# First layer's router scores by rows: the turned rows of a tile standing, the router's eight columns moving

## The reference

```python
def _L0_ffn_ref(X, routing_W, expert_bias, sW1, sb1, sW2, sb2, rW1, rb1, rW2, rb2):
    shared = jax.nn.silu(X @ sW1 + sb1) @ sW2 + sb2
    logits = jnp.einsum('btd,ed->bte', X, routing_W) + expert_bias
    activation = jnp.sqrt(jax.nn.softplus(logits))
    top_vals, top_idx = jax.lax.top_k(activation, K)          # K = 2
    ...
    hdn = jax.nn.silu(jnp.einsum('nd,edh->enh', Xf, rW1) + rb1[:, None, :])
    y = jnp.einsum('enh,ehd->end', hdn, rW2) + rb2[:, None, :]
    routed = jnp.einsum('ne,end->nd', cf, y).reshape(B, T, d)
    return shared + routed

x = x + _L0_xattn_ref(ctx_1024, _layernorm(x), ...)
x = x + _L0_ffn_ref(_layernorm(x), ...)
x = x + _L1_xattn_ref(_layernorm(x), ctx_1024, ctx_1024, ...)
x = x + _L1_ffn_ref(_layernorm(x), ...)
```

## Time and profile before

| | us |
|---|---|
| median of 3 runs | 826.47 |
| the three runs | 830.29, 826.28, 826.47 |
| span of the profiled execution | 827.7 |
| PE busy | 767.8 (93%) |
| PE weight loads busy | 662.7 (80%) |
| DVE busy | 501.6 (61%) |
| ACT busy | 487.8 (59%) |
| POOL busy | 424.7 (51%) |
| score products, 16 recorded in the first stretch | 7.5 busy |
| ACT copies of the scores, 8 | 0.59 each |

### The profile page before, as it was taken

How to read it: one execution, slowest core, us unless ns; L and a number is a source line. 1 busy time by engine, 2 the same in 40 slices (tenths; PEclk the granted TensorE clock), 3 DMA queues, 4 the chain that set the end, 5 groups by cost and what they waited for, 6 DMA issues and landing times.

```text
span 827.7 us, 16421 instructions
## 1 busy us (share of the span) xinstructions
PE 767.8 (93%) x4472; PEld 662.7 (80%) x4472; DVE 501.6 (61%) x1360; ACT 487.8 (59%) x1374; POOL 424.7 (51%) x399
## 2 busy tenths in 40 slices
PE   4899997989898599999999999789999999999998
PEld 3646645767776499999998998679999999999997
DVE  5777856652666388788888978676222222244236
ACT  2437746655566578888778787354444444444442
POOL 3000765555686767888655788534552354322221
PEclk9989999999999899999999999899999999999999
DMA  8999996887799973553620434613444433355347
GB/s 257 345 297 336 324 312 218 263 250 222 174 251 215 299 210 84 133 123 85 177 63 1 134 136 147 201 56 116 136 135 142 134 104 103 104 181 185 121 144 232
DMA packets 128362, 147.94 MB, mean 179 GB/s; under 512 B 10747, under 2 KB 120214, under 8 KB 127254
## 3 DMA queue, kind: packets, MB, share of 16 engines
q1 hardware_dynamic: 102512, 106.02, 42.1%
q0 software_dynamic: 18624, 34.29, 15.7%
q10 hardware_dynamic: 7142, 6.59, 2.5%
HBM read 73.46 MB, written 73.40 MB: 177 GB/s over the span
## 4 chain that ended last, share of the span: by engine, by line
PE 73%; DVE 12%; DMA 4%; ACT 4%; issue 3%; DVEq 2%; SPq 0%; POOL 0%; ACTq 0%; POOLq 0%
PE psum L806 26%; PE psum L1096 9%; PE psum L1118 9%; PE psum L1184 6%; PE psum L1189 6%; PE psum L1185 6%; PE psum L1106 3%; PE psum L1198 3%; DMA fx<-xs_dram 2%; ACT pr L1485 2%; PE psum L1166 2%; PE psum L992 2%; DVE xstats L1665 1%; DVE prl L2227 1%; PE psum L1080 1%
## 5 line engine op out<-in xcount | busy, mean ns | idle before, releaser
L726 POOL DMA_INDIRECT yk_dram<-ys,L x52 | 52.1, 1003 | 144.6 <-ACT ys L1558 144.5
L673 POOL DMA_INDIRECT X<-yl_dram,slots_y x64 | 101.2, 1581 | 37.7 <-issue 13.3
L2308 DVE TENSOR_TENSOR hs<-psum,hs 128x384 f32<-128x384 f32 x71 | 39.7, 559 | 125.1 <-PE psum L1189 119.1
L645 POOL DMA_INDIRECT xs_dram<-N,slots x64 | 65.5, 1023 | 95.9 <-DVEq L1858 58.8
L1485 ACT ACTIVATE pr<-psum,nmx 128x64 f32<-128x64 f32 x512 | 108.4, 364 | 9.1 <-DVE nmx L2212 9.0
L1184 PE MATMUL psum<-whi,xTh 128*128 x284 | 109.7, 386 | 2.2 <-ACT xTh L1538 2.2
L806 PE MATMUL psum<-w_sb,cz 128*128 x426 | 103.7, 380 | 0.6 <-ACT ys L1558 0.4
L1185 PE MATMUL psum<-wlo,xTh 128*128 x284 | 96.0, 338 | 0.0
L714 POOL DMA_INDIRECT xs_dram<-N,slots x64 | 66.9, 1045 | 40.0 <-ACT ys L1558 23.3
L806 PEld LDWEIGHTS psum<-w_sb,cz 128*128 128x128 f32 x426 | 75.5, 190 | 8.4 <-issue 1.0
L1189 PE MATMUL psum<-whi,xTl 128*128 x284 | 74.0, 341 | 1.8 <-DVE xTl L2331 1.8
(11 more groups left out here) (360 smaller groups left out, 1850.1 us busy)
## 6 DMA issues: line engine op xcount, KB each, us to landing
fx<-xs_dram SPq DMA_DIRECT2D x80, 130.0 KB, 3.4
xs_dram<-fill SPq DMA_DIRECT2D x4, 2600.0 KB, 15.9
yl_dram<-fy SPq DMA_DIRECT2D x80, 128.0 KB, 3.2
xs<-xs_dram SPq DMA_DIRECT2D x71, 130.0 KB, 2.1
wlo<-in_L_ffn_W_dram SPq DMA_DIRECT2D x4, 1536.0 KB, 8.3
xs_dram<-cz SPq DMA_DIRECT2D x1, 5200.0 KB, 21.3
xs_dram<-cz SPq DMA_DIRECT2D x8, 650.0 KB, 6.7
X<-in_x_dram SPq DMA_DIRECT2D x4, 1024.0 KB, 11.9
```

The source lines that it names most:

```text
L645: po.indirect_dma_start(XS, bass.IndirectOffsetOnAxis(ap=slot[k][:, t:t + 1], axis=0), N0[:, t, :], None).then_inc(s[done], 16)
L673: po.indirect_dma_start(X[:, t, :], None, YL[b // 2], bass.IndirectOffsetOnAxis(ap=slot_y[k][:, t:t + 1], axis=0), compute_op=ALU.add).the ...
L726: po.indirect_dma_start(YK, bass.IndirectOffsetOnAxis(ap=yid[:, j:j + 1], axis=0), ys[j % YB], None).then_inc(s[f"y_out{j % YB}"], 16)
```

## The change

In `scores(g)` on TensorE the two operands change places. For each of a quad's four tiles and each half of the 256 numbers, the 128x128 turned rows stand and the 8 columns of the router move; the result is 128 partitions x 8 columns, written at once to the tile's columns of bank 4. `turn`, the ACT function `logits` with its copies and the buffer lgT0 are gone, and with them the semaphores l_lg and l_lt. The products of quad q raise l_tn, on which `choose(g)` waits as it did. Two waits of the sends get other semaphores.

```diff
@@ gpsimd: send @@
                     if (k, t) == (1, 4):
-                        po.wait_ge(s["l_lt"], LQ + 2)
+                        po.wait_ge(s["l_xa"], LQ + 3)
                     if (k, t) == (1, 8):
-                        po.wait_ge(s["l_lt"], 2 * LQ)
+                        po.wait_ge(s["l_tn"], 2 * LQ)
@@ tensor: scores @@
-                def turn(q):
-                    pe.wait_ge(s["l_lt"], q + 1)
-                    for t in range(QT):
-                        u = q * QT + t
-                        last = nc.tensor.transpose(bank[4][:, u * E:u * E + E], lgT0[q % 2][:, t * P:t * P + P], ident[0:E, 0:E])
-                    last.then_inc(s["l_tn"], 1)
...
                     pe.wait_ge(s["l_xa"], q + 1)
                     pe.wait_ge(s["l_xd"], q + 1)
-                    if q >= q0 + 2:
-                        pe.wait_ge(s["l_lt"], q - 1)
-                    for c in range(DC):
-                        last = mm(bank[3 + 2 * (q % 2)][0:E, :], roT[0][:, c, :], xT4[:, q % LQ, c, :], c == 0, c == DC - 1)
-                    last.then_inc(s["l_lg"], 1)
-                    if q > q0:
-                        turn(q - 1)
-                turn(q0 + LQ - 1)
+                    for t in range(QT):
+                        u = q * QT + t
+                        for c in range(DC):
+                            last = mm(bank[4][:, u * E:u * E + E], xT4[:, q % LQ, c, t * P:t * P + P], roT[0][:, c, :], c == 0, c == DC - 1)
+                    last.then_inc(s["l_tn"], 1)
@@ scalar: scores @@
-                def logits(q):
-                    ac.wait_ge(s["l_lg"], q + 1)
-                    if q >= 2:
-                        ac.wait_ge(s["l_tn"], q - 1)
-                    act(lgT0[q % 2], bank[3 + 2 * (q % 2)][0:E, :], ACT.Copy).then_inc(s["l_lt"], 1)
...
-                    if q > q0:
-                        logits(q - 1)
-                logits(q0 + LQ - 1)
```

More of the change, by code:

```diff
@@ L194, in build @@
         convw_sb = sb("convw_sb", [P, RATE, DC, D], stack=s1)[:, :, :, :]
-        lgT0 = [convw_sb[0:E, k, :, :].rearrange("p c n -> p (c n)") for k in range(2)]
         cu = sb("cu", [P, 2, 2, D], stack=s1)
@@ L294, in build @@
             b2_in b2_lo b2_zero sw_in rw_in
-            l_sa l_sb l_sc2 l_w2 y_back y_late l_nr l_tp l_xa l_xd l_lg l_lt l_tn l_ev l_su l_hs l_sy l_xu
+            l_sa l_sb l_sc2 l_w2 y_back y_late l_nr l_tp l_xa l_xd l_tn l_ev l_su l_hs l_sy l_xu
             f_tp f_xt f_h f_hs f_y f_ys
```

## The result

The changed kernel takes 831.59 us (median of 20 runs, 828.26 to 833.95) where the kernel before takes 828.42 us (20 runs, 823.84 to 835.27) on the same chip. The ratio is 1.0041, 95% interval 1.0026 to 1.0056: 3.4 us slower, near the 830.8 us forecast. That is within the half per cent that I took as no change, but the interval lies above 1, so the loss is clear of the noise. The time of the kernel before rests here on 20 runs; the first three of them, from which I started, had a median 2 us lower.

The account below looks back on a forecast made before the run. TensorE, busy 93% of 827.7 us, was taken as the bound. With its clock falling, 2.4 + 1.1 + 0.8 = +4.3 us on the 826.47 us median gave 830.8 us, range 822.8 to 835.5.

Parts of the forecast that it names:

- The clock falls behind narrow products: Main case, chance 0.50: TensorE's clock halves in both score stretches, +4.3 us, giving 830.8 us.
- The cost of +2.4 us: First score stretch: clock falls before the last quad's turnings, L at 68.0 instead of 65.63 us (+2.4 to +0.9).
- The full-clock prices: Score stretches at full clock: product block 1.76 us; L 1.53 us earlier in the first, 1.98 in the second.
- rival 2: Score products: clock holds but strided columns cost 0.15 us each, 2.4 us a block; +0.3 us, 826.8 us; chance 0.05.
- The second stretch: Second score stretch: clock falls over the last two blocks, -1.98 + 3.04 = +1.1 us (-2.0 to +3.5).
- the term at the rank product: Behind the second score stretch: 3.5 us of low clock, of which about 0.8 us reach VectorE.
- the one said to be hidden: Low clock behind the first score stretch: costs nothing, hidden by 1.06 us of TensorE idle before the second.
- Queues: Sends behind the second choice land in busier DMA queues and lose 0.3 us of the gain (0 to 1.1).
- rival 1: Both score stretches: TensorE's clock holds, L comes earlier twice, -3.2 us, 823.3 us (822.5 to 824.5); chance 0.30.

Follow-up runs that it names:

- c2: The changed kernel, with no further edit, run and profiled again on one chip with the kernel before; ratio 1.0036 against the kernel before.
- e1: The changed kernel with each score product moving the router's 8 columns sixteen times over (128 columns); ratio 0.9979 against the kernel before.
- e7: The same kernel as e1 (changed kernel, 128 columns moving), run again in another group; ratio 0.9992 against the kernel before.
- e5: The changed kernel with each score product moving the router's 8 columns four times over (32 columns); ratio 1.0020 against the kernel before.
- c1: The kernel before, unchanged, run and profiled again as a control; ratio 0.9988 against the other runs of the kernel before.
- e8: The kernel before with two of eight 650 KB zero fills issued after the first six loads of expert rows; ratio 1.0032 against the kernel before.
- e9: e7 with two of eight zero fills issued after the first six loads of expert rows; ratio 1.0020 against the kernel before.
- e6: The kernel before with new products only for each score stretch's last quad, 128 columns moving; ratio 0.9993 against the kernel before.
- e4: The kernel before with new products, 8 columns moving, only for the last quad of each score stretch; ratio 0.9956 against the kernel before.
- e10: The same kernel as e4 (new products only for each stretch's last quad), run again in another group; ratio 0.9967 against the kernel before.

## Why the prediction came out as it did

**The clock falls behind narrow products: right.** It was the likeliest case, at 0.50. L in the first stretch was put at 68.0 us, 16.2 behind the first turning; it came at 68.40, 15.9 behind, and 15.7 in c2. The cost of +2.4 us measured +2.1 and +1.9. That how much moves decides, which I had argued from the earlier trace rows alone, is shown by e1, e7 and the second stretch of c2. By the idle-gap rule of the Trainium skill ("TensorE: Matmul & The Clock Gate", "HAM oscillation") alone the clock would have held there; the trace disagrees, with PE busy 7.00 of 7.00 us ahead of c2's fall at 119.2 us.

**The full-clock prices: right.** Where the clock held, in after's second stretch, L came 11.02 us behind the first turning, 2.4 less than before. I had summed -1.98 for an unchanged start; the 0.4 us more are half at the front of the stretch, where the first products start 2.00 us behind the first turning in place of 2.23, and half in the turnings, of which eight take 0.91 us behind narrow products (115.03 to 115.94) in place of 1.02. The strided columns bring a block to 1.81 us from start to start (113.22 to 115.03), close to the 1.76 of the sum and far from the 2.4 of rival 2, which falls.

**The second stretch: mis-sized.** The term was +1.1 us (the fall covers the last two blocks). It measured -2.4 in one profile and -0.4 in the other: the fall came right behind the stretch, or within the first of the last two blocks. The range of -2.0 to +3.5 had the place open; I chose a middle that lay 1.5 to 3.5 us too high.

**Behind the stretches: the term at the rank product right, the one said to be hidden wrong.** The 0.8 us for the rank product measured 0.5 and 1.7. The keys and values behind the first stretch ran at the low clock until 74.2 us, and I called that hidden by the 1.06 us of idle in the earlier trace rows. In after it was not: the rank product stood at 74.73, the second stretch began 0.9 us later behind its L, released by ACT and not by VectorE. In c2, whose fall was 3.4 us shorter, it was hidden (+0.03).

**Queues: the term that was too small.** I gave 0.3 us (0 to 1.1) for sends that land in busier queues. The wait that took their place is the first load of sent rows, which is issued when the last send has landed. The DMA share by stretch, before and then after:

```profile
76.00:80.00 4.00, 4.00 (x17) 2.76 (x16) 3.18 (x15) 3.66 (x8) 0.00 (x0) 1.00 1.11 356
...
132.00:134.00 2.00, 2.00 (x7) 1.03 (x6) 1.48 (x8) 1.65 (x2) 0.00 (x0) 1.00 0.13 30
```

```profile
76.00:80.00 4.00, 4.00 (x18) 3.19 (x17) 3.52 (x12) 3.90 (x7) 0.00 (x0) 1.00 0.41 138
...
132.00:134.00 2.00, 1.28 (x7) 1.21 (x8) 1.64 (x7) 1.06 (x3) 0.96 (x1) 1.00 1.01 410
```

Two things meet here. The engines that move data are nearly full until about 128 us in the kernel before, and the low clock behind the first stretch starved them for once: 138 GB/s in place of 356 from 76 to 80 us, since the stores wait for copies of products that PE made late (the store queue waited 6.4 us for one copy, 2.4 at most before). What was not moved then is moved at the end, where the queues run full until 134 us. Before, the first load was issued 11.7 us behind L; after, 14.6; c2 13.7; e5 15.2; e7 15.9. In before, 1.6 us of PE's idle time stood ahead of the first expert product, and a load that comes later than that is paid: 2.0 us in e5, 0.4 in after. In c2 PE reached the loads late by itself: it had waited 2.01 us for ysh, as in after (0.91 before), and fell to the low clock once more at 136.3 us, which makes the 1.5 us of that step.

Counted from the start of the last send, the two causes come apart. The load is issued 2.5 to 2.9 us behind it in before, c1, c2, e1, e8 and e9, and 4.8 to 6.1 us behind it in after, e5, e6 and e7. So in c2 the load is late because the sends are; in after and e5 it is late behind the sends, with the queues full. e6 shows the second cause without the first: it has no fall of the clock up to there and lies on the chip of the result, but everything in it comes early, since the clock had not fallen near 44 us either. Its last send starts at 128.1 us and its first load at 133.2 (before: 130.1 and 132.6), and PE waits for it:

```profile
135.38 0.96 PE L1000 MATMUL psum<-ident,fx 128*128 128x128 f32 x4 [2.24 <-DMA fx<-xs_dram]
```

When the sends come early, the backlog does not end earlier. That speaks against the full -3.2 us of rival 1 even at full clock. The ratios can't say: e1 and e7, which had nearly the low clock of the kernel before, came out 0.2% and 0.1% below it, within their uncertainty, and their second stretches were disturbed.

**The sum.** Forecast +4.3 us on a base of 826.47, measured +3.4 us (2.2 to 4.6) on 828.42. The steps up to the first expert product give +1.5 and +4.8 in the two pairs, so two profiles do not fix which terms make up the +3.4. The forecast of the change was 0.9 us too high and the base 2 us too low; the second stretch was too dear, and the late load and the late start of the second stretch, which I had nearly at nothing, made up for part of it. That the total came so close is in part luck.

## What to carry to other kernels

Turning a product round so that 8 columns move and 128 stand can save time by the instruction and lose it by the clock: look at what is fed to TensorE per weight load over the whole stretch, and count what follows the stretch at half speed too. In these runs such products paid, if anywhere, where a copy and a turning back end the path, with dense work around them (e4, e10). And before a gain ahead of a load is counted, look whether the DMA engines are full there: in e6 and e7 the sends came earlier and the backlog did not end earlier.

## What the runs showed that I had not expected

A block of 32 columns behind a 128-column load takes the same time as one of 8 (1.94 and 1.92 us for 16), and lost the clock in the same place of the first stretch. In the second it kept it (1.00 from 108 to 132 us), where after lost it at 122.0 and c2 at 119.2 us.

On two of three chips the kernel before was 1.6 and 2.0% slower (842 and 846 us against 829), and in the profiles there, semaphores from TensorE came late in the busiest DMA stretch. In e1 the row turnings of two quads are recorded as done by 109.9 us, and the copies that wait for them alone start at 110.72, and at 114.35:

```profile
107.57 2.29 PE L898 MATMUL psum<-ident,N 128*128 128x128 f32 x16 [1.09 <-issue]
...
110.72 0.60 ACT L1319 ACTIVATE xT<-psum 128x512 f32<-128x512 f32 x1 [1.99 <-PE psum L898]
114.35 0.60 ACT L1319 ACTIVATE xT<-psum 128x512 f32<-128x512 f32 x1 [3.03 <-remote]
```

VectorE's copies of the same quads start at the same two moments. The page names the second releaser only as "remote". On the chip of the result such copies start within 0.3 us of the turnings' end. What delays them was not tested. It is in the old kernel's order too (e8), but no ratio can be cleared of it, and it made the second stretches of seven profiles unreadable.

The granted clock also falls at places that no edit touched, and not in every execution (near 44 us in some profiles of one kernel and not in others, e1 and e7), which moves the first turning between 49 and 53 us. A single profile's span therefore tells nothing about a change of 3 us. The distance between two marks inside it tells more: it repeated to 0.01 us in the kernel before, though in the changed kernel, where the fall moves, the same distances differ by 0.2 to 2 us.
